# Scattering the last experts' results in the order of tokens while the experts run, on one Trainium2 core

## The reference, cut to what matters

```python
def _L1_ffn_ref(x, Wr, Wg, Wu, Wd, Sg, Su, Sd):       # E, K, F = 16, 2, 128; FS = 256
    xf = x.reshape(T, d)
    shared = jax.nn.silu(xf @ Sg) * (xf @ Su) @ Sd
    probs = jax.nn.softmax(xf @ Wr, axis=-1)
    topk_p, topk_i = jax.lax.top_k(probs, K)
    cw = jnp.zeros((T, n_exp), x.dtype).at[jnp.arange(T)[:, None], topk_i].add(topk_p)
    def step(acc, ew):
        wg, wu, wd, c = ew
        y = jax.nn.silu(xf @ wg) * (xf @ wu) @ wd
        return (acc + y * c[:, None], None)
    routed, _ = jax.lax.scan(step, jnp.zeros_like(xf), (Wg, Wu, Wd, cw.T))
    return (routed + shared).reshape(b, s, d)
...
x = x + _L1_ffn_ref(_layernorm(x, axis=-1), ...)      # once before the attention, once after it, as the last block
return x
```

## Time and profile before

| | |
|---|---|
| median of 3 runs | 5039.34 us |
| lowest and highest run | 5037.54 and 5043.3 us |
| the profiled execution's span, from its first to its last instruction | 5046.6 us |
| what lies around the span in that execution | not in the page |
| busy: PE, DVE, ACT, POOL | 3946.2, 2845.7, 2217.0, 2475.4 us |
| DMA, mean over the span | 94 GB/s |
| last experts' loop, from its first gather to its last result | 4806.49 to 4952.05 us |
| last part, from its first gather to the end | 4954.91 to 5046.6 us |

### The profile page before, as it was taken

How to read it: one execution, slowest core, us unless ns; L and a number is a source line. 1 busy time by engine, 2 the same in 40 slices (tenths; PEclk the granted TensorE clock), 3 DMA queues, 4 the chain that set the end, 5 groups by cost and what they waited for, 6 DMA issues and landing times.

```text
span 5046.6 us, 49393 instructions
## 1 busy us (share of the span) xinstructions
PE 3946.2 (78%) x15216; PEld 2274.4 (45%) x15218; DVE 2845.7 (56%) x4948; ACT 2217.0 (44%) x4098; POOL 2475.4 (49%) x2152
## 2 busy tenths in 40 slices
PE   6888888759947778897788769977965788887892
PEld 2333333347724445675333346645642333333671
DVE  6999999941146664211888842236334666554422
ACT  5566666321147664112555533333334444445241
POOL 5999999822212333111888944433455311112256
PEclk9999999959968888998888879987986799999896
DMA  5666665422210100321555521123347222211145
GB/s 152 158 161 151 161 160 159 127 77 85 84 56 17 34 26 9 105 102 53 150 153 145 145 82 46 44 90 94 92 131 154 72 40 39 39 27 46 46 137 131
DMA packets 312121, 476.73 MB, mean 94 GB/s; under 512 B 34890, under 2 KB 167990, under 8 KB 311786
## 3 DMA queue, kind: packets, MB, share of 16 engines
q1 hardware_dynamic: 277152, 388.87, 29.1%
q0 software_dynamic: 29184, 76.12, 5.4%
q10 hardware_dynamic: 5504, 8.39, 0.6%
HBM read 375.26 MB, written 97.49 MB: 94 GB/s over the span
## 4 chain that ended last, share of the span: by engine, by line
PE 39%; POOL 7%; DVE 6%; issue 5%; ACT 4%; DMA 3%; SPq 0%; DVEq 0%; ACTq 0%; POOLq 0%; another core or an unknown queue 0%
PE s_gate_up L2305 8%; PE s_result_sum L2321 4%; PE s_out_sum L3676 3%; PE s_hidden_sum L1745 3%; PE s_result_sum L1756 3%; PE s_scores_T L3660 3%; POOL s_h L435 2%; PE s_shared L2961 2%; DVE s_maxima L3308 2%; PE s_scores L3617 2%; POOL s_gathered L1047 1%; PE s_shared L2971 1%; POOL s_h L444 1%; PE s_transposed L2295 1%; PE s_mid_transposed L2314 1%
## 5 line engine op out<-in xcount | busy, mean ns | idle before, releaser
L435 POOL TENSOR_TENSOR s_h<-s_dtu,s_bc 128x1024 f32<-128x1024 f32 x384 | 904.0, 2363 | 78.4 <-PE s_y_sum L477 61.9
L477 PE MATMUL s_y_sum<-s_h,identity 128*128 128x512 f32 x1536 | 776.3, 643 | 158.2 <-POOL s_h L444 150.4
L402 ACT ACTIVATE s_decay<-s_dt,s_A 128x512 f32<-128x512 f32 x768 | 498.3, 681 | 330.2 <-DVE s_h L377 323.4
L477 PEld LDWEIGHTS s_y_sum<-s_h,identity 128*128 128x128 f32 x1536 | 296.5, 203 | 600.4 <-issue 305.3
L3482 ACT ACTIVATE s_weights_T<-s_scores_T 128x1024 f32<-128x1024 f32 (+3 forms) x384 | 292.2, 809 | 311.9 <-PE s_scores_T L3660 309.7
L2305 PE MATMUL s_gate_up<-s_w_gate_up,s_rowsT 128*128 x1184 | 420.5, 488 | 2.8 <-issue 2.4
L3308 DVE TENSOR_REDUCE s_maxima<-s_scores 128x1 f32<-128x512 f32 (+3 forms) x440 | 282.6, 659 | 218.7 <-PE s_scores L3621 140.0
L444 POOL TENSOR_TENSOR s_h<-s_h,s_bc 128x512 f32<-128x512 f32 x288 | 367.1, 1275 | 23.6 <-DVE s_h L370 14.9
L3530 POOL TENSOR_SCALAR_AFFINE_SELECT s_weights_T<-s_weights_T 128x256 f32<-128x256 f32 x256 | 103.2, 408 | 541.2 <-ACT s_weights_T L3482 538.6
L2364 DVE TENSOR_TENSOR s_mid<-s_act,s_gate_up 128x128 f32<-128x128 f32 (+1 forms) x228 | 92.9, 407 | 454.7 <-ACT s_act L2337 430.2
L370 DVE TENSOR_TENSOR_SCAN s_decay<-s_decay,s_carry,s_h 128x512 f32<-128x512 f32 x240 | 303.1, 1276 | 24.5 <-POOL s_clip_flag L2633 13.8
(11 more groups left out here) (533 smaller groups left out, 7739.6 us busy)
## 6 DMA issues: line engine op xcount, KB each, us to landing
s_bc<-s_bc_rows SPq DMA_DIRECT2D x384, 512.0 KB
sorted_results<-s_result SPq DMA_DIRECT2D x160, 128.0 KB
s_w_inter<-in_L_ffn_experts_inter SPq DMA_DIRECT2D x16, 1024.0 KB
s_w_exp_out<-in_L_ffn_experts_out SPq DMA_DIRECT2D x16, 1024.0 KB
s_queries<-parts_of_q SPq DMA_DIRECT2D x96, 128.0 KB
s_keys<-parts_of_k SPq DMA_DIRECT2D x96, 128.0 KB
results_by_token<-zeros SPq DMA_DIRECT2D x16, 512.0 KB, 6.1
s_pair<-results_by_token SPq DMA_DIRECT2D x16, 512.0 KB
```

The costliest lines, as they stand in the source:

```text
L402: S.e.activation(self.decay[:, (2 * g + d) % 4, :], dt[q // self.passes % 2][:, at, :], ACT.Exp, scale=A[:, at, g % ns:g % ns + 1]).then_i ...
L435: G.e.tensor_tensor(self.h[r][:], dtu[q // self.passes % 2][:, at:at + 2, :], mid(self.bc[r][:, 0, :], 2), ALU.mult).then_inc(*self.fed.up())
L477: made = T.e.matmul(self.y[:, d, :], ident[:], self.h[r][:, d, :], start=False, stop=g % ns == ns - 1)
```

## The change

moe1b, the last stage, asks its table for `results_at` and its experts for the scatter on POOL in place of SP's plain stores; moe1a stays as it was. `result_stage` loads the two planes of all eight chunks plainly on SP, each chunk into buffers of its own, adds them on DVE, and SP stores the chunks behind all the loads. An import line moves every later line down by one (L2283 becomes L2284, L2380 becomes L2381).

```diff
-def moe1_stage(K, W):
+def moe1_stage(K, W, by_planes=False):
...
-                      R.work[:].rearrange("p a n -> p (a n)").bitcast(BF16))
+                      R.work[:].rearrange("p a n -> p (a n)").bitcast(BF16), planes=by_planes)
...
-    tiles = ExpertTiles(K, M, R.tile_expert, R.routed.at(1), E, F, w_gu, w_d, banks)
-    tiles.sync()
+    tiles = ExpertTiles(K, M, R.tile_expert, R.routed.at(1), E, F, w_gu, w_d, banks,
+                        results_at=table.results_at if by_planes else None)
+    if not by_planes:
+        tiles.sync()
...
-    K.owed, K.kept = "plain", None
+    K.owed, K.kept = "planes" if by_planes else "plain", None
...
-          "rwkv": rwkv_stage, "ssm1": ssm1_stage, "moe1a": moe1_stage, "moe1b": moe1_stage,
+          "rwkv": rwkv_stage, "ssm1": ssm1_stage, "moe1a": moe1_stage, "moe1b": functools.partial(moe1_stage, by_planes=True),
...
 def result_stage(K, out_tiles):
+    V, Q = K.V, K.Q
     M = Memory(K)
-    stored = K.event(16, "dma")
-    if K.owed is not None:
-        combine = Combine(K, M, K.X, 2 * TPC, TPC)
-        combine.gpsimd_gather(2 * TPC)
+    got = [[M.sb(f"planes{c}_{i}", [P, TPC, D]) for i in range(2)] for c in range(NC)]
+    stored, here, added = K.event(16, "dma"), K.events(NC, 32, "dma"), K.events(2)
+    by_token = K.planes.rearrange("(i t p) c -> i p t c", i=2, p=P)
     for c in range(NC):
-        if K.owed is not None:
-            combine.vector_add(c)
-            K.Q.wait_ge(*combine.chunk_added(c))
-            combine.gpsimd_gather(TPC)
-        K.Q.e.dma_start(out_tiles[:, chunk_tiles(c), :], K.X[:, chunk_tiles(c), :]).then_inc(*stored.dma())
-    K.Q.wait_ge(*stored.now())
+        for i in range(2):
+            Q.e.dma_start(got[c][i][:], by_token[i][:, chunk_tiles(c), :]).then_inc(*here[c].dma())
+    for c in range(NC):
+        V.wait_ge(*here[c].now())
+        for i in range(2):
+            V.wait_ge(*added[0].at(c if i else c - 1))
+            for j in range(TPC):
+                t = TPC * c + j
+                made = V.e.scalar_tensor_tensor(K.X[:, t, :], got[c][i][:, j, :], K.pick_weight[i][:, t:t + 1],
+                                                K.X[:, t, :], ALU.mult, ALU.add)
+            made.then_inc(*added[i].up())
+    for c in range(NC):
+        Q.wait_ge(*added[1].at(c))
+        Q.e.dma_start(out_tiles[:, chunk_tiles(c), :], K.X[:, chunk_tiles(c), :]).then_inc(*stored.dma())
+    Q.wait_ge(*stored.now())
     K.barrier()
     M.free()
```

More of the change, by code:

```diff
@@ L1 @@
+import functools
 import itertools
```

## The result

The changed kernel takes 5058.78 us (median of 7 runs, 5050.79 to 5066.41). The kernel before, run beside it, takes 5039.73. The ratio is 1.0034, with a 95% interval of 1.0023 to 1.0045: 17 us slower (19 between the two medians). The forecast was 5065, the range 5050 to 5081.

The account below looks back on a forecast made before the run. PE was taken to bound the last experts' loop and POOL's gathers the last part. The loop's 71.6 us more minus the last part's 46.0 less gave 25.6 over 5039.3, so 5065, range 5050 to 5081.

Parts of the forecast that it names:

- POOL becomes the loop's bound: Last experts' loop: a gather and scatter pair takes 2.69 us on POOL (2.58 to 2.73), over PE's 1.64 a tile.
- my two ways: Estimates of a POOL gather and scatter pair: 1.38 + (1.03 + 0.30) = 2.71 us, or 1.38 + 1.28 = 2.66.
- The last scatter: Loop's end: 73 pairs take 196.4 us, then final gather, PE rounds and copy; last scatter starts at about 5023.4.
- The hand-over to the last part: From the last scatter's start to SP's first load: 3.10 us, so loads start at 5026.5, 71.6 later than the old gathers.
- The table of places: Three small VectorE operations and one flag more before the first gather: costs nothing; without cover 0.7 us.
- The last part: 64 gathers replaced by plain loads at 298 GB/s with stores behind: 45.7 us against 91.7, 46.0 less.
- The sum: Whole kernel: 71.6 - 46.0 = 25.6 us more, a median of 5065; main case 5051 to 5075.
- Rival A: Loop: a scatter's issue costs nearly nothing, the loop keeps 1.64 us a tile; 45 us less, 4994; chance 0.04.
- Rival B: Loop: PE's waits drop its granted clock to 0.5, 3.28 us a tile; 43 us more, 5108; chance 0.06.
- Rival C: Loop: scattered rows land late and ACT waits for result buffers; at 13 us landing 59 us more, 5124; chance 0.03.
- Rival D: Whole kernel: pairs at 2.58 us, transfers at 348 GB/s and another small saving; about +8 us, 5047; chance 0.05.

Follow-up runs that it names:

- two half changes: Kernel before with only the new last part (results stored plainly): 4987.92 us, ratio 0.9901; with only the scattering loop and old last part: 5113.53 us, 1.0153.
- eight buffers: Changed kernel with eight row and eight result buffers instead of four in the last experts' loop: 5102.71 us, ratio 1.0108 (stalled); repeated on another chip 5059.68, 1.0033.
- sorted-in version: Changed kernel with the loop's 80 gathers replaced by 64 earlier POOL scatters of token rows and plain SP loads: 5045.07 us, ratio 0.9988; repeated 5004.99, 0.9921.

## Why the prediction was right, step by step

**POOL becomes the loop's bound.** Right. A pair was put at 2.69 us between 2.58 and 2.73; it measured 194.04 / 73 = 2.658 from scatter 0 to scatter 73 (4803.91 to 4997.95), which is the second of my two ways (1.38 + 1.28). The error in the first way was the row: ssm1's gather to scatter step of 1.38 contains a gather of 1.07, and here the same step is 1.34.

**The last scatter at 216.9 us after the first gather.** It measured 5008.29 - 4791.38 = 216.9, but two errors cancel in this agreement. Scatter 0 came 12.5 us after the first gather, not 12.1, and scatter 73 at 206.6, not 208.5. The tail from there took 10.3 us in place of 8.4, and PE and ACT set it, not POOL. The last gather's rows were transposed 4.0 us after its start where 3.1 was put (5000.61 - 4996.62), from there to the end of the last copy it took 6.9 us in place of 6.3 (5007.52 - 5000.61), and the scatters stood waiting for ACT:
```profile
4996.62 1.02 POOL L2284 DMA_INDIRECT s_rows<-rows_by_token,s_rows_at  x1 [0.30 <-issue]
...
5000.61 0.44 PE L2296 MATMUL s_transposed<-identity,s_rows 128*128 128x128 f32 x2 [0.53 <-DMA s_rows<-rows_by_token,s_rows_at]
...
5001.27 0.98 POOL L2381 DMA_INDIRECT results_by_token<-s_result,s_results_at  x1 [1.00 <-ACT s_result L2354]
...
5004.27 0.99 POOL L2381 DMA_INDIRECT results_by_token<-s_result,s_results_at  x1 [2.02 <-ACT s_result L2354]
...
5007.14 0.38 ACT L2354 ACTIVATE s_result<-s_result_sum 128x256 f32<-128x256 f32 x1 [0.98 <-PE s_result_sum L2322]
```
So the agreement to 0.1 us is luck; the parts were off by up to 2.4 us, in both directions.

**The hand-over to the last part.** Put at 3.10 us from the earlier trace rows, measured 5010.83 - 5008.29 = 2.54: 0.56 less.

**The table of places.** Costed at nothing, and right as far as the traces show. From SP's first load of the stage (the router's weights) to the first gather it takes 163.0 us before (4806.49 - 4643.48) and 163.0 in the second execution of the change (4807.92 - 4644.97). In the first one it was 166.2 (4791.38 - 4625.19), but these 3.2 us are there 18 us after the routing's start, before the table is built, and beside them PE's granted clock was 0.68 over the routing's first ten us, 0.84 in the other. They lie ahead of the first gather and are not in the 17.5.

**The last part.** This is the mis-sized term: 45.7 us predicted, 38.2 measured, 7.5 less. The structure was right: loads at a full line, the stores behind the loads, DVE between. (DVE needs 3.3 us for a chunk, and a chunk's loads now only 3.0, so it worked without a pause and ended at 5043.03, 32.2 us after the first load's issue; 33.7 was put.) The rate was not right: 349 GB/s for the loads, 369 and 385 where the stores join, in place of 298. The error was in my reading of the earlier trace rows, and the trace of before holds the answer. The same loads in narrower stretches:
```profile
3370.00:3371.00 1.00, 0.00 (x0) 0.00 (x0) 0.00 (x0) 0.00 (x0) 0.00 (x0) 0.50 0.54 87
3371.00:3379.00 8.00, 0.00 (x0) 0.00 (x0) 3.34 (x8) 0.91 (x4) 0.00 (x0) 0.50 1.08 346
3379.00:3380.00 1.00, 0.00 (x0) 0.00 (x0) 0.00 (x0) 0.94 (x5) 0.00 (x0) 0.50 0.92 135
```
The stretches of 5 us had mixed the loads at their rate, 346, with their slow first microsecond and with a dip between two groups of loads. The start was even counted twice, once in the 303 and once as 2.1 us of latency. With 346 the 12.58 MB take 36.4 us in place of 42.2, and the last part comes to 39.9, 1.7 over the measured one. The bound on that side, 6.1 less, was passed by 1.4, since the stores ran above 348. The Trainium skill's 358 GB/s for a core's share of HBM (DMA: Bandwidth & Descriptors, Where 436 GB/s comes from) lay nearer than my 298. The trace passes it as well, with 385 in one stretch. The same page (Bandwidth, Measured) gives up to 425 GB/s for a core whose neighbour is idle, and the trace agrees in so far as the rate goes above the share; 425 was not reached in any stretch here. The prediction's remark that the rows of this case stay below 358 holds only for the stretches of 5 us that it shows.

**The sum.** 25.6 predicted; 25.6 - 7.5 - 0.56 = 17.5, which is what the traces show between the first gather and the end. The median came out 6 us under the 5065. The two half changes show its parts: +71.0 for the loop (predicted 71.6) and -54.3 for the last part (predicted -46.0; 7.5 of the 8.3 between them are the last part's, mostly the rate).

**Rival A, the scatter hides.** Refuted: 65 of the 80 scatters start 0.3 us behind the instruction before them, with nothing but issue between. The Trainium skill's "small, variable" for a descriptor's generation (DMA: Bandwidth & Descriptors, Anatomy of one DMA) can't be taken as the cost of an indirect DMA: here it is 1.02 us busy and 0.30 of issue each. What the page says of emitting many descriptors before the cost shows agrees if it is read of the rows in one DMA: half of them bought only 0.1 us.

**Rival B, the clock.** Refuted for this kernel: the granted clock is 1.00 in the five stretches of 40 us from 4802 to 5002, with PE busy 30.5 to 32.1 of 40 us. I had expected 24. The same 720 PE instructions count 166.61 busy us in place of 138.31. About 8 of these 28 us are longer records (gate and up 91.3 us in all in place of 86.6, the transposes 35.2 in place of 31.7); the other 20 are overlap, since the records of neighbouring instructions overlap when PE runs through and less when it waits between them. So the busy share taken over from the old profile was too low by nearly a quarter. A busy share alone doesn't tell the clock either: in the stalled kernel with eight buffers PE was busy for 31.48 of 40 us in the stretch shown above, at a granted clock of 0.76 and with 115 records in place of some 139.

**Rival C, landing and result buffers.** Refuted by the eight buffers, and by a loop in which no wait of ACT names a scatter. The scatters landed 2.5 us (median) after their issue; C needed some 9.

**Rival D, a draw.** Half right: the last part was as short as it said, but the pairs weren't 2.58.

## What to carry to other kernels

Cost an indirect DMA by its engine's step, here 1.3 us each with 128 rows and 1.2 with 64, and put it where that engine has room: here a change that took 83 us off a bare last part lost, since it put 105 into a loop with room for 42, and the same idea won 0.8% once the loop's gathers had been moved beside other work. Where two halves of a change can be built apart, their local sum (first changed instruction to the end) tells more than the medians when the stages ahead vary by 10 us. When a rate is read from stretches, take them narrow enough to leave out the start and the pauses. And before a strange wait is given a mechanism, repeat the kernel beside a known one on another chip.

## What the runs showed of the hardware that I had not expected

- POOL's time for an indirect DMA hardly depends on its rows: in the experts' loop a scatter takes 1.02 us with 128, 0.93 with 64 and 0.98 for the last ones, some of which hold no row. In the sorted-in version, where scatter follows scatter, 128 rows take 0.97.
- Some of POOL's scatters are slower while DVE builds the table. In the sorted-in version two of them:
```profile
4770.17 1.56 POOL L2944 DMA_INDIRECT sorted_results<-s_xn,pick_row  x1 [0.30 <-issue]
...
4776.46 0.97 POOL L2944 DMA_INDIRECT sorted_results<-s_xn,pick_row  x1 [0.30 <-issue]
```
  The first starts while DVE works on the table (operations at 4770.07 and 4770.81), the second between two operations of DVE. Seven of the 64 take 1.54 to 1.57 us, 0.6 more, and all seven overlap operations of DVE for the routing or the table. The overlap alone is not enough: the scatter at 4768.89 runs beside one of them too and takes 0.97. The Trainium skill says that the two engines share their interfaces to SBUF and contend for some DVE instructions (GPSIMD Engine Reference, Specifications); the trace agrees with that, but what sets the slow ones apart is not shown.
- TensorE's granted clock stayed at 1.00, its upper level of 2.4 GHz, from 4802 to 5002, 200 us in which PE's weight loads waited for rows in most tiles. In the stalled kernel with eight buffers it was 0.76 to 0.91 in stretches of 40 us of the same loop.
- On one chip, in two kernels, engines stood still for up to 21 us with their work ready, under waits that the profile lists as remote, and both came out some 40 us longer than on the next chip. What it was stays open.
